# The first attention's step on TensorE: paired scores in the three-bank steps, and one tile fewer for GpSimd in every other unit

## The reference, cut to what matters

```python
q = _qdq(x) @ _qdq(wq).T + bq          # x is layer-normed
kv = cond @ wkv.T + bkv                # cond is ctx_2048
attn = softmax(einsum('bnhd,bmhd->bhnm', q, k) / sqrt(Dh), axis=-1)
o = einsum('bhnm,bmhd->bnhd', attn, v)
out = _qdq(o) @ _qdq(wp).T + bp
```

## Time and profile before

| what | value |
|---|---|
| runs, us | 2577.19, 2578.29, 2578.38 (median 2578.29) |
| profiled execution, its own time | 2578.61 us |
| its span | 2576.8 us |
| granted TensorE clock, mean | 0.996 |
| span from the first S to the last S of this stage | 628.7 to 1388.4 us |
| L1473 GpSimd, 140 + 16 adds | 640.7 + 73.3 us, 4576 ns each |
| L1334 ScalarE exp, 832 | 458.3 us, 598 ns each |
| L1361 VectorE maxima, 480 | 455.1 us, 988 ns each |
| L1226 TensorE scores, 832 | 333.0 us |
| L1191 TensorE windows, 960 matmuls | 265.4 us |

### The profile page before, as it was taken

How to read it: one execution, slowest core, us unless ns; L and a number is a source line. 1 busy time by engine, 2 the same in 40 slices (tenths; PEclk the granted TensorE clock), 3 DMA queues, 4 the chain that set the end, 5 groups by cost and what they waited for, 6 DMA issues and landing times. The chain is left out here.

```text
span 2576.8 us, 33913 instructions
## 1 busy us (share of the span) xinstructions
PE 2514.3 (98%) x13273; PEld 1624.6 (63%) x13288; DVE 1790.2 (69%) x2456; ACT 1232.3 (48%) x1853; POOL 1287.2 (50%) x340
## 2 busy tenths in 40 slices
PE   8999999999999999999999999999999999999998
PEld 8988888987545545545444787888533333335786
DVE  4554544556767767767774676664799999999873
ACT  4222312311666666666664232222588888886110
POOL 0000000001999999999993000000499999997310
PEclk9999999999999999999999999999999999999999
DMA  8677776655545345344313754542997777776400
GB/s 302 212 253 239 266 276 242 217 178 157 114 87 112 72 93 111 68 97 106 68 67 118 259 188 135 175 156 85 253 213 162 167 160 167 156 172 193 125 33 33
DMA packets 218864, 405.10 MB, mean 157 GB/s; under 512 B 18216, under 2 KB 94536, under 8 KB 218640
## 3 DMA queue, kind: packets, MB, share of 16 engines
q1 hardware_dynamic: 218704, 402.93, 56.6%
HBM read 260.63 MB, written 140.59 MB: 156 GB/s over the span
## 5 line engine op out<-in xcount | busy, mean ns | idle before, releaser
L1473 POOL TENSOR_TENSOR pooled<-pooled,probs 128x2048 f32<-128x2048 f32 x140 | 640.7, 4576 | 21.0 <-ACT probs L1334 0.9
L1334 ACT ACTIVATE probs<-psum 128x512 f32<-128x512 f32 (+1 forms) x832 | 458.3, 598 | 334.9 <-PE psum L1226 330.1
L1361 DVE TENSOR_REDUCE win_max<-psum 128x1 f32<-128x802 f32 x480 | 455.1, 988 | 150.5 <-PE psum L1191 150.5
L2258 DVE TENSOR_SCALAR probs<-psum,bound 128x1024 f32<-128x1024 f32 (+1 forms) x416 | 498.8, 1275 | 31.0 <-POOL pooled L2290 21.3
L2233 ACT ACTIVATE probs<-probs 128x1024 f32<-128x1024 f32 (+1 forms) x416 | 437.5, 1059 | 81.9 <-DVE probs L2258 39.6
L2290 POOL TENSOR_TENSOR pooled<-pooled,probs 128x2048 f32<-128x2048 f32 x92 | 424.2, 4611 | 12.8 <-ACT probs L2233 0.4
L1226 PE MATMUL psum<-q_st,k_st 128*128 128x512 f32 (+1 forms) x832 | 333.0, 437 | 18.7 <-ACT probs L1334 12.2
L312 POOL TENSOR_TENSOR r_q<-ve_q,minus_half 128x4 f32<-128x4 f32 x8 | 9.1, 1132 | 611.2 <-DVE ve_q L256 611.2
L1226 PEld LDWEIGHTS psum<-q_st,k_st 128*128 128x128 f32 (+1 forms) x832 | 148.4, 185 | 241.2 <-ACT probs L1334 179.9
L1191 PE MATMUL psum<-k_st,q_st 96*128 96x402 f32 x960 | 265.4, 358 | 6.6 <-DVE o_sb L1380 5.0
L2201 PE MATMUL psum<-q_st,k_st 128*128 128x512 f32 (+1 forms) x832 | 252.7, 430 | 10.1 <-DVE probs L2258 7.8
(11 more groups left out here) (276 smaller groups left out, 4217.1 us busy)
## 6 DMA issues: line engine op xcount, KB each, us to landing
k_st<-k_hi SPq DMA_DIRECT2D x64, 801.0 KB, 10.4
k_st<-k_lo SPq DMA_DIRECT2D x48, 801.0 KB, 10.8
k_hi<-kt_hi SPq DMA_DIRECT2D x32, 801.0 KB
k_lo<-kt_lo SPq DMA_DIRECT2D x32, 801.0 KB
v_rows<-v_out SPq DMA_DIRECT2D x96, 256.0 KB
v_st<-v_rows SPq DMA_DIRECT2D x24, 768.0 KB
q_st<-q_hi SPq DMA_DIRECT2D x64, 256.0 KB, 7.7
w<-w_hi_d SPq DMA_DIRECT2D x64, 256.0 KB, 3.1
```

Of the source, the lines that this page charges most:

```text
L1334: A.activation(probs[i % NPROBS][0:rows, j, :], bank(score_banks.where["score", u, t, j])[0:rows, :], ACT.Exp, scale=1.0 / ROOT).then_inc( ...
L1361: V.tensor_reduce(win_max[:, r, j, c:c + 1], window(windows.where["max", u, i])[:, :, 0:MV], AX.XY, ALU.max).then_inc(max_done, 1)
L1473: G.tensor_tensor(pooled[u % 2][:], before[:], probs[tile(u, k) % NPROBS][:], ALU.add).then_inc(pool_added, 1)
L2258: V.tensor_scalar(probs[i % NPROBS][0:rows, half * W:half * W + W, :], window(("score", u, t, half))[0:rows], bound[0:rows, u // NG, t:t + 1],
```

## The change

Four edits. The third bank is used from step 4 instead of 5. `pooled_tiles` is 11 in even units and 10 in odd ones (7 in the last). In the steps with three banks TensorE's order changes from S0 M0 S1 M1 V S2 M2 S3 to M0 S0 S1 M1 V M2 S2 S3; and C and T, which stood after S3, now stand straight after V in every unit. VectorE does the closing of step 4 between its second and third maximum instead of after the third.

```diff
--- before.py
+++ after.py
@@ -1147,7 +1147,7 @@
                     return (u - 1) * HPG * RT * 2 + i
 
                 def three_banks(u, t):
-                    return 5 <= t < pooled_tiles(u) + LAG
+                    return 4 <= t < pooled_tiles(u) + LAG
 
                 def window_of(i):
                     j, rest = divmod(i, RT * 2)
@@ -1159,7 +1159,7 @@
 
                 def pooled_tiles(u):
 
-                    return 11 if u < UNITS - 1 else 7
+                    return 11 - u % 2 if u < UNITS - 1 else 7
 
                 def kq_count(u):
 
@@ -1290,10 +1290,13 @@
 
                     for now, behind in steps():
                         coming = [(now[0] + 1, i) for i in windows_at(now[1])] if now and now[0] + 1 < UNITS else []
-                        if now:
+                        paired = now and three_banks(*now)
+                        if now and not paired:
                             scores(*now, 0)
                         if coming:
                             max_of(*coming[0])
+                        if paired:
+                            scores(*now, 0)
                         if now:
                             scores(*now, 1)
                         if coming[1:]:
@@ -1303,15 +1306,18 @@
                             if behind[1] == LAST_SUM and behind[0]:
                                 last_sum(behind[0] - 1)
                         if now:
-                            scores(*now, 2)
-                        if coming[2:]:
-                            max_of(*coming[2])
-                        if now:
-                            scores(*now, 3)
                             if now[1] == CLOSE_AT and now[0]:
                                 closing(now[0] - 1)
                             if now[1] == TURN_AT and now[0] + 1 < UNITS:
                                 turn(now[0] + 1)
+                            if not paired:
+                                scores(*now, 2)
+                        if coming[2:]:
+                            max_of(*coming[2])
+                        if now:
+                            if paired:
+                                scores(*now, 2)
+                            scores(*now, 3)
                             if now == (UNITS - 2, TURN_AT):
                                 quantising()
                             if now == (UNITS - 1, CODES_AT):
@@ -1437,11 +1443,13 @@
                     V.memset(ones[:], 1.0).then_inc(set_up, 1)
                     V.wait_ge(own.sem, s)
                     for now, behind in steps():
-                        if now and now[0] + 1 < UNITS:
-                            for i in windows_at(now[1]):
-                                max_of(now[0] + 1, i)
+                        coming = [(now[0] + 1, i) for i in windows_at(now[1])] if now and now[0] + 1 < UNITS else []
+                        for one in coming[:2]:
+                            max_of(*one)
                         if now and now[1] == CLOSE_AT and now[0]:
                             closing(now[0] - 1)
+                        for one in coming[2:]:
+                            max_of(*one)
                         if now and now[1] == TURN_AT - 1 and now[0] + 1 < UNITS:
                             turn(now[0] + 1)
                         if now == (UNITS - 2, TURN_AT - 1):
```

## The result

The changed kernel took 2593.73 us in the median of 4 runs (2592.53 to 2596.44) against 2578.34 of the kernel before: a ratio of 1.0056, 95% interval 1.0044 to 1.0069 (an estimate from the runs; the bare quotient of the two medians is 1.0060). It is slower, by 15.4 us; 2594 was forecast. The profiled execution took 2593.99 us with a span of 2592.2.

The account below looks back on a forecast made before the run. TensorE, chained with ScalarE's exps and VectorE's maxima, was taken as the bound, GpSimd having slack. Odd units +13.0, even +2.8, unit 14 +0.4, unit 0 -0.6, unit 15 +0.5: +16.1 us, so 2594; range 2580 to 2603.

Parts of the forecast that it names:

- Part 1: Paired order in three-bank steps: period 3.35 us instead of 3.51, five periods, 0.80 us a unit won.
- The exps' gate: On TensorE, from a score through ScalarE's exp to the bank's release: 1.08 us, expected to hold S1 in paired steps.
- the maxima's: Gate on TensorE from M2's start through VectorE's maximum to the slot's release: 1.61 us, holding M1 before the change.
- the 0.10: Extra time in us that a group on TensorE takes right behind V or behind a wait.
- The content rival: Paired steps run without any wait, 3.22 us instead of 3.35: 10 us less, 2584 us; chance 0.2.
- Part 2: Third bank in step 4: S0 waits for the copy of the sums; with the closing, 0.80 us a unit lost.
- Part 3: T ahead of S2 delays S2, its exp, S1 and V of step 12: 0.36 us a unit lost.
- Part 4: End of even units: with 36 three-bank scores, next unit's S0 takes the preceding S2's bank: 0.11 us lost.
- Part 5: Ten tiles in odd units: an extra D on TensorE and a two-bank step 12, 1.49 us a unit lost.
- The ends: First and last units, reckoned apart: unit 0 at -0.6 us, unit 15 at +0.5 us.
- the closing's term: Between V of step 4 and V of step 5, M0 waits for VectorE's closing: 0.10 us lost.
- As the bound: Rival that GpSimd's adds set the pace: 2561 us, or about 2570; chance 0.11 with other ways for gates not biting.

Follow-up runs that it names:

- pairs_alone: The kernel before with only the paired order in three-bank steps (third bank from step 5, eleven tiles, C and T behind S3): 2566.00 us.
- bank_at_5: The changed kernel with the third bank used from step 5 again: 2580.39 us.
- den_free: The changed kernel with S0 and S1 of step 4 kept on banks 0 and 1, bank 7 joining from S2 of step 4: 2579.41 us.
- c_t_back: The changed kernel with C and T behind S3 again and the closing last on VectorE in step 4: 2587.69 us.
- tens_alone: The kernel before with only ten tiles on GpSimd in odd units: 2586.35 us.
- eleven: The changed kernel with 11 tiles on GpSimd in every unit but the last: 2585.25 us.
- c_after_m2: pairs_alone with C between M2 and S3 of step 4: 2567.95 us.
- phase: pairs_alone with bank 7 used for scores from S2 of step 4 in eleven-tile units: 2569.53 us.
- v_early: pairs_alone with V between S0 and S1 in the three-bank steps: 2589.78 us.
- c_after_m2_ten: c_after_m2 with ten tiles on GpSimd in unit 0 alone: 2566.80 us.
- phase_tens: The kernel before with the edits of pairs_alone, c_after_m2 and phase, and ten tiles on GpSimd in units 0, 5 and 10: 2561.47 us.

## Why the prediction was right

- **Part 1, the paired order.** -0.80 a unit forecast, five periods of 3.35 instead of 3.51. Measured 3.35, and pairs_alone won 12.4 us of the stage. The exps' gate at S1 took the place of the maxima's, as walked: in the steady step of the changed kernel S1's weight load idles 0.24 us for ScalarE (956.16) and M1's starts without idle time (956.32). The content rival (3.22) did not come. One row was misread on the way, without harm to the sum: the 0.41 us at 888.57 are idle time of the weight loads. M1 itself, 0.23 behind S1 at 888.15, could have started at 888.38 and came 0.19 late; with the 0.10 behind it that is the 0.29 between 3.22 and 3.51. The 253 and 79 waits of the earlier trace rows are idle times of the loads too, with the 0.84 us behind each V among them, and not so many waits of the matmuls.
- **Part 2, the third bank in step 4.** +0.80 forecast as 0.71 for the wait and 0.10 for the closing. Measured from V of step 3 (930.25) to V of step 5 (940.20) 9.95 against 9.20: +0.75, all but 0.01 of it the wait. The closing's step was oversized by 0.09: M0 came 2.31 behind C (936.42 to 938.73) where 2.35 was put, V 1.47 behind M0 where 1.51 was put. M1's load did wait 0.23 us for M2's maximum, as walked, but its matmul came only 0.01 later for it. bank_at_5 and den_free both take this loss away in ways of their own.
- **Part 3, T ahead of S2.** 0.36 forecast, 0.38 measured; c_t_back returns it.
- **Part 4, the banks' turn in even units.** 0.11 forecast; 3.40 before, 3.51 to 3.54 after, so 0.11 to 0.14.
- **Part 5, ten tiles.** 1.49 forecast for the odd units' end; 0.48 (3.43 against 2.95) and 0.99 (4.39 against 3.40) measured, 1.47.
- **The ends.** Unit 0: -0.6 forecast, -0.6 measured. Unit 15: +0.5 forecast, +0.9 measured: C in step 4 gave 0.44, and a turn of the banks at step 8 to 9 (2.62 to 3.09), which I had not counted there, another 0.47.
- **The sum.** +16.1 forecast, +15.4 in the stage and in the medians: +12.3 in the seven odd units (13.0 forecast), +2.5 in the even ones from 2 to 12 (2.8), +0.3 in unit 14 (0.4), -0.6 in unit 0 and +0.9 in unit 15 (0.5). The mechanism and the terms are right to within 0.1 a unit. That the time came within 0.3 us of 2594 is better than they are: the closing's term was 1.2 us too large over 14 units, the turn of the banks missed in unit 15 gave 0.5 back, and the four runs themselves spread over 3.9 us.
- **GpSimd.** As the bound it was wrong for the kernels before and changed (tens_alone is slower, eleven faster than the changed one), but its 0.8 us of slack was just the 0.8 that the pairs won: with them alone it has none, and what is won beyond runs into it (c_after_m2, phase). In the changed kernel its idle time at a unit's start grew by 6.4 us after odd units (0.82 to 7.24), where 6 was forecast, but by about 0.4 after even ones (to 1.20 to 1.28), where 1 was.
- **The 0.10 behind a wait.** In v_early as in the kernel before the gated window takes 0.10 more (894.76 to 895.24 is 0.48 against 0.37 unhindered), and the forecast period of 3.35 was met with it in it. Around the closing it was put in three times, at C, M0 and M1, and came out as 0.06, 0.11 and 0.06.

## What to carry to other kernels

Before a resource with several uses is handed out earlier, ask which instruction will take it first and what that one must wait for; on TensorE here all that was queued behind paid, with V 0.72 late for one wait of 0.81 us. With buffers taken in turn, count the uses modulo the number of buffers. Where the number of buffers changes, here from three banks to two, the remainder decides which wait is met: 34 scores instead of 32 before that point made a unit 0.5 us shorter, 36 made it 0.1 longer. Taking work off an engine that has slack costs what the other engine pays for it; first win the time that uses up the slack, then relieve it in as few places as the floor demands.

## What the runs showed of the hardware that I had not expected

The stretch with TensorE's wait for GpSimd in unit 15 of phase cost more than the wait. Step 3 to 4 is 8.82, 4.09 more than in pairs_alone. Of these, 2.46 are last_sum's later start behind V (2.27 of idle time in its row), and 1.63 lie between its start and the next V, in work that is the same in both kernels. There the granted clock is lower, in the profile's table by stretches (columns: stretch, then its length, busy time of PE, PEld, DVE, ACT and POOL, granted clock, DMA share, GB/s):

```profile
1335.00:1340.00 5.00, 4.06 (x16) 1.40 (x16) 1.68 (x2) 3.74 (x8) 4.57 (x2) 1.00 0.00 2
1340.00:1345.00 5.00, 2.73 (x17) 0.31 (x16) 0.00 (x0) 0.99 (x2) 5.00 (x2) 0.88 0.00 0
1345.00:1350.00 5.00, 5.00 (x32) 3.30 (x28) 2.22 (x2) 2.61 (x5) 4.86 (x2) 0.78 0.01 3
1350.00:1355.00 5.00, 4.93 (x32) 2.66 (x30) 1.08 (x3) 3.31 (x7) 4.86 (x2) 1.00 0.17 52
```

The clock is granted in full, 2.4 GHz, until 1340 and from 1350 on, and in a part of the time between at the half, 1.2 GHz: means of 0.88 and 0.78. The eight matmuls of L1259 take 1.74 there and 1.04 at the same place in pairs_alone. That this wait is followed by such a stretch is seen; that it is the cause is not shown, and c_after_m2 speaks for caution: at the same place TensorE idles 1.97 us for GpSimd, the clock stays at 1.00, and the step pays 2.16 us and no more.

The time outside the stage was not quite constant: span less stage is 1822.1 before and after and 1821.0 to 1823.5 in the other kernels, but 1824.4 in c_after_m2_ten and 1825.2 in phase_tens, so that of the 18.5 us won in the stage of phase_tens 15.4 arrive in the span. Of the missing 3.1 us, 1.3 lie ahead of the stage, where the code is the same (the first V starts at 637.05, before at 635.78), and 1.7 in the first 20 us behind it. There the granted clock is lower for longer than in pairs_alone; the first row is of phase_tens, the second of pairs_alone:

```profile
1380.00:1400.00 20.00, 18.05 (x74) 14.42 (x74) 8.61 (x15) 6.39 (x10) 0.00 (x0) 0.83 1.01 361
...
1380.00:1400.00 20.00, 15.95 (x82) 12.07 (x75) 8.10 (x14) 7.16 (x11) 0.00 (x0) 0.91 0.75 259
```

Both may come and go from one execution to the next: the four runs of phase_tens took 2559.18, 2559.68, 2563.26 and 2563.27 us, and the profiled one is the longest. Whether the two shorter ones lacked these 3 us no trace shows.
